# DLRM tower on one core: the first 32 samples prepared tile by tile with factors from TensorE, gathers and weight loads reordered

## What is computed

```python
def _cin_layer(X0, Xi, W, b):            # W: (128, 39 * Fi)
    Wr = W.reshape(H, F0_, Fi)
    return jnp.einsum('hjk,bjd,bkd->bhd', Wr, X0, Xi) + b[None, :, None]
Xi = X0 = e
for W, b in Ws:                          # three layers of 128 maps
    Xi = _cin_layer(X0, Xi, W, b)
    res.append(Xi.sum(axis=2))
z = jnp.concatenate(res, axis=1)         # (512, 384)
h = jnp.concatenate([z, dense_ctx], axis=1)
h = jnp.maximum(h @ W_top1 + b_top1, 0.0)   # 400 x 512
h = jnp.maximum(h @ W_top2 + b_top2, 0.0)   # 512 x 256
y = h @ W_top3                              # 256 x 1
```

## Time and profile before

| | |
|---|---|
| median of 3 runs | 688.73 us (688.02 to 689.34) |
| the profiled execution | 685.9 us, span 684.0 us, mean granted clock 0.99 |
| PE / PEld busy | 94% / 74% |
| DVE / ACT / POOL busy | 82% / 65% / 68% |
| HBM read | 8.86 MB |

### The profile page before, as it was taken

One profiled execution on the slowest core, in us unless ns is written; L12 is line 12 of the kernel. 1 busy time (PEld: TensorE's weight loads), 2 busy tenths in 40 slices (PEclk: granted clock), 3 DMA queues, 4 the chain that ended last, 5 costly groups with the idle time before them and its releaser, 6 DMA issues.

```text
span 684.0 us, 10984 instructions
## 1 busy us (share of the span) xinstructions
PE 641.0 (94%) x2920; PEld 507.6 (74%) x2920; DVE 558.1 (82%) x1560; ACT 441.3 (65%) x1434; POOL 464.6 (68%) x372
## 2 busy tenths in 40 slices
PE   0069999999999999999999999999999999999997
PEld 0037777777778877777788877877778887777877
DVE  4149999999994599999995589999997489999860
ACT  4026877777773477777684477778685377777751
POOL 6746888888874478787886368787886377444440
PEclk9999999999999999999999999999999999999988
DMA  6146424031312102213131200403040300300000
GB/s 217 41 128 242 149 67 122 11 109 24 97 36 80 52 3 56 79 35 99 27 107 27 95 13 18 115 19 115 18 117 16 102 17 14 117 2 5 1 1 1
DMA packets 39057, 44.35 MB, mean 65 GB/s; under 512 B 17427, under 2 KB 22253, under 8 KB 38867
## 3 DMA queue, kind: packets, MB, share of 16 engines
q1 hardware_dynamic: 33363, 42.34, 20.3%
q0 software_dynamic: 5632, 1.31, 2.1%
HBM read 8.86 MB, written 0.00 MB: 13 GB/s over the span
## 4 chain that ended last, share of the span: by engine, by line
PE 92%; DMA 2%; POOL 2%; SPq 1%; ACT 1%; issue 1%; DVE 1%; DVEq 0%
PE p_u L606 22%; PE p_u L608 21%; PE p_u L607 21%; PE p_tower L625 6%; PE p_x L583 6%; PE p_g L616 5%; PE p_x L580 2%; PE p_x L577 2%; PE p_x L578 2%; POOL emb L277 2%; PE p_tower L652 1%; DMA fac_b<-xx 1%; PE p_tower L638 1%; PE p_tower L637 1%; PE p_x L562 1%
## 5 line engine op out<-in xcount | busy, mean ns | idle before, releaser
L362 ACT ACTIVATE prod<-p_u,x0t 128x128 f32<-128x128 f32 x1024 | 289.3, 375 | 91.3 <-PE p_u L608 91.0
L496 DVE SCALAR_TENSOR_TENSOR parts<-p_u,x0t,parts 128x128 f32<-128x128 f32 x1024 | 283.0, 339 | 41.5 <-PE p_u L608 41.5
L606 PE MATMUL p_u<-w1h,x1h 128*128 128x512 f32 (+1 forms) x640 | 286.6, 448 | 2.3 <-DVE x1l L473 2.3
L608 PE MATMUL p_u<-w1h,x1l 128*128 128x512 f32 (+1 forms) x640 | 250.2, 391 | 0.0
L607 PE MATMUL p_u<-w1l,x1h 128*128 128x512 f32 (+1 forms) x640 | 249.9, 390 | 0.0
L277 POOL DMA_INDIRECT emb<-table_in,idx_all x176 | 204.5, 1162 | 51.4 <-issue 47.8
L296 POOL TENSOR_TENSOR parts<-parts,prod 128x512 f32<-128x512 f32 x128 | 176.3, 1378 | 57.8 <-ACT prod L362 44.2
L606 PEld LDWEIGHTS p_u<-w1h,x1h 128*128 128x128 f32 x640 | 121.0, 189 | 38.4 <-issue 9.7
L607 PEld LDWEIGHTS p_u<-w1l,x1h 128*128 128x128 f32 x640 | 121.6, 190 | 35.4 <-issue 10.1
L291 POOL TENSOR_TENSOR parts<-prod 128x512 f32<-128x512 f32 x64 | 83.6, 1306 | 86.8 <-ACT prod L362 86.1
L608 PEld LDWEIGHTS p_u<-w1h,x1l 128*128 128x128 f32 x640 | 120.6, 188 | 26.1
(11 more groups left out here) (56 smaller groups left out, 346.9 us busy)
## 6 DMA issues: line engine op xcount, KB each, us to landing
fac_b<-xx SPq DMA_DIRECT2D x96, 234.0 KB
fac_a<-xx SPq DMA_DIRECT2D x48, 78.0 KB
emb<-table_in,idx_all POOLq DMA_INDIRECT x176, 2.8
g_all<-w_in SPq DMA_DIRECT2D x3, 832.0 KB, 9.6
xx<-xx SPq DMA_DIRECT2D x32, 78.0 KB
fac_b<-xx SPq DMA_DIRECT2D x16, 156.0 KB
w<-w_in SPq DMA_DIRECT2D x1, 2496.0 KB, 10.2
bd<-x0t SPq DMA_DIRECT2D x128, 10.0 KB
```

The costliest lines, as they stand in the source:

```text
L362: last = nc.scalar.activation(dst[:, i * H:(i + 1) * H], u[:, i * H:(i + 1) * H], ACT.Copy, scale=x0t[:, par, t, j:j + 1])
L496: nc.vector.scalar_tensor_tensor(out=chain[i][:, p], in0=u[:, i * H:(i + 1) * H], scalar=x0t[:, par, t, j:j + 1], in1=add, op0=ALU.mult, o ...
L606: nc.tensor.matmul(u, xh, wh, start=True, stop=False)
L608: nc.tensor.matmul(u, xl, wh, start=False, stop=True).then_inc(u_full, 1)
```

## The change

Group 0 is prepared one tile at a time, and in another sample order (gather g holds samples 3g, 3g + 1, 3g + 2 of the group in its three parts, so that three gathers complete the first tile). TensorE moves the rows (`first_x0_rows`) and makes the factors by matmuls with selection matrices `rep`, `rep_a` (`first_factors`); DVE multiplies straight out of PSUM (`first_products`), and layer 0 runs on 128 columns in plain fp32 (`first_layer0`). Tile 0 is prepared ahead of the loop, tile t + 1 at fixed quads of tile t. The identity and the selection matrices are loaded from ACT's queue. W1 is asked for once the first three gathers have landed, in parts from its end, and the quads of a tile run through the fields from the end.

Group 1 is prepared at slots 30 to 39 of group 0, all in plain fp32. Group 2's gathers go into the loop: 6, 5, 3, 4 behind the four tiles of group 0, three behind each tile of group 1, then 3, 3, 3, 2. `bd` of group 0 is filled in two steps. The top network's weights are asked for after `spread(2)` and `place_bd(1)`. The context is loaded in group 0's sample order, and `y` is put back into order by three more copies.

The core of the diff:

```diff
+FIRST_PARTS = [range(0, 3), range(3, 6), range(6, 8), range(8, GATHERS)]
+F_X0, F_X0_OUT, F_PICK, F_PICK_OUT, F_XT_OUT, F_LAYER0, F_X1 = 0, 1, 3, 4, 5, 7, 7
+F_G = 8
+F_S_COLUMNS = 30
+F_S_PAIR = [30 + k for k in range(GROUPS)]
+F_S_ADD = [32 + k for k in range(GROUPS)]
+F_S_X1, F_S_X1L, F_S_Z1 = 38, 39, 31
+F_S_W0 = 16
+GATHER_ORDER = [(M, g) for M in range(2, MACROS * BLOCKS) for g in range(GATHERS)]
+GATHER_QUOTA = [6, 5, 3, 4] + [3] * 4 + [3, 3, 3, 2] * (MACROS * BLOCKS - 2)
-QUAD_J = [list(range(36, 39))] + [list(range(4 * q, 4 * q + 4)) for q in range(9)]
+QUAD_J = [list(range(36, 39))] + [list(range(4 * q, 4 * q + 4)) for q in reversed(range(9))]
...
             sp.dma_start(base[:], base_d).then_inc(idx_in, 16)
-            sp.dma_start(eye[:], eye_d).then_inc(eye_in, 16)
             sp.dma_start(fac_b[:].rearrange("p k c -> p (k c)")[:, 0:2 * GROUPS * H], w0_d).then_inc(w0_in, 16)
+            sp.wait_ge(first_in[0], 16 * len(FIRST_PARTS[0]))
             step = F * H // W1_PARTS
             for i in range(W1_PARTS):
+                c = slice((W1_PARTS - 1 - i) * step, (W1_PARTS - i) * step)
+                sp.dma_start(w1_raw[:, c], w1_d[:, c]).then_inc(w1_in[i], 16)
-            spread(0, 0, first=True)
+            sp.wait_ge(bd_cleared, 1)
+            sp.wait_ge(f_xt_made, 2)
+            place_first_bd(0, f_bd_in)
             spread(1, 1)
+            sp.wait_ge(f_xt_made, TILES)
+            place_first_bd(2, bd_in[0])
             over_blocks(body)
...
             pool.wait_ge(idx_made, 1)
-            for M in (0, 1):
-                for g in range(GATHERS):
-                    gather(M, g)
-            for g in range(8):
-                gather(2, g)
+            for t in range(TILES):
+                for g in FIRST_PARTS[t]:
+                    gather(0, g, first_in[t])
+            for g in range(GATHERS):
+                gather(1, g, gathered[1])
...
+            def first_x0_rows(t):
+                for i in range(t + 1):
+                    pe.wait_ge(first_in[i], 16 * len(FIRST_PARTS[i]))
+                need(pe, f_x1f_made, t)
+                o = p_x1[0:F, t * 128:(t + 1) * 128].rearrange("p (s d) -> p s d", d=D)
+                for c in range(STACK):
+                    last = nc.tensor.matmul(o[:, s0:TILE_B:STACK, :], eye[0:(c + 1) * F, c * F:(c + 1) * F],
+                                            emb[0:(c + 1) * F, 0, g0 * D:g1 * D].rearrange("p (g d) -> p g d", d=D),
+                                            start=True, stop=True)
+            def first_factors(t):
+                x0 = first_x0[:, t * 128:(t + 1) * 128]
+                pe.wait_ge(f_x0_made, t + 1)
+                need(pe, f_z_made, 2 * t)
+                nc.tensor.matmul(p_x1[0:ROWS, t * 128:(t + 1) * 128], rep_a[:], x0,
+                                 start=True, stop=True).then_inc(f_a_full, 1)
+                for k in range(GROUPS):
+                    last = nc.tensor.matmul(o, rep[:, k:k + ROWS], x0, start=True, stop=True)
+                    if k in (3, GROUPS - 1):
+                        last.then_inc(f_b_full, 1)
+                pe.wait_ge(f_a_made, t + 1)
+                nc.tensor.transpose(p_x1[:, t * 128:t * 128 + F], x0, eye[0:F, 0:F]).then_inc(f_xt_full, 1)
+            def first_layer0(t):
+                pe.wait_ge(f_xt_made, t + 1)
+                for k in range(GROUPS):
+                    if k in (0, 4):
+                        pe.wait_ge(f_z_made, 2 * t + (2 if k else 1))
+                    rows = GROUP_ROWS[k]
+                    last = nc.tensor.matmul(p_x1[:, t * 128:(t + 1) * 128], w0[0:rows, k * H:(k + 1) * H],
+                                            first_z0[0:rows, k, :], start=(k == 0), stop=(k == GROUPS - 1))
+                last.then_inc(f_l0_full, 1)
...
+            def first_products(t):
+                dve.wait_ge(f_a_made, t + 1)
+                need(dve, f_l0_full, t)
+                for bank, ks in ((p_g, range(0, 4)), (p_tower, range(4, GROUPS))):
+                    dve.wait_ge(f_b_full, 2 * t + (2 if ks[0] else 1))
+                    nc.vector.tensor_tensor(out=first_z0[:, ks[0]:ks[0] + n, :],
+                                            in0=bank[0:ROWS, 0:n * 128].rearrange("p (k c) -> p k c", c=128),
+                                            in1=fac_a[:, 0:1, c].to_broadcast([ROWS, n, 128]),
+                                            op=ALU.mult).then_inc(f_z_made, 1)
...
+            first_columns(0)
+            first_factor(0)
+            first_x0t(0)
+            w1_high(0)
+            w1_high(1)
+            first_x1(0)
+            w1_high(2)
...
+            first_products(0)
+            w1_low(0)
+            first_x1l(0)
+            w1_low(1)
+            w1_low(2)
...
+            first_x0_rows(0)
+            pe.wait_ge(rep_a_made, STACK)
+            first_factors(0)
+            pe.wait_ge(w0_summed, 1)
+            first_layer0(0)
             over_blocks(body)
```

317 lines of the change are left out of this document (215 added, 102 removed).

## The result

The changed kernel takes 683.94 us in the median of 9 runs (680.01 to 687.67), the kernel before 688.73 on the same chip (9 runs, 687.58 to 689.34). The ratio is 0.9935, 95% interval 0.991 to 0.9961: faster by 4.8 us, where 11.7 were forecast. The runs of after spread over 7.7 us, those of before over 1.8. The profiled execution of after is the slowest of the nine, so it shows the losses at their largest. The ratios in this document leave out the few executions that took over 1.5% longer than the fastest of the same kernel; the medians are of all.

A forecast was written before the change was run, and what follows sets the result against it. TensorE bounds the steady groups, so only the 49 us head could be won. Group 1 at 72.5 instead of 84.73 gains 12.2: 685.9 - 12.2 + 0.5 = 674.2 profiled, 677.0 as median, range 671.5 to 684.5.

The forecast's parts named there:

- What bounds the kernel: Whole kernel: TensorE has no gap from 84.73 us on, groups take 35.35; only the 49 us head can be won.
- rival (b): Group 0: TensorE bounds it, small matmuls cost up to 0.41 us, group 1 starts at 75 to 80.5, 680 to 685; chance 0.17.
- The prediction's own signs of being wrong: First quad after 25 us, tiles 1 and 2 over 14, clock of 20 to 70 below 0.9, or later groups over 35.4.
- Start of the quads: Head: W1's transfer and rounding set quad 0 at about 18.9 us instead of 49.06, bounds 18 and 21.
- The price of the small matmuls: Group 0: 0.22 us each, plus 0.8 us per tile for possible mode changes, 4.7 us per tile taken.
- 1.5 for a start at half clock: Tile 0 of group 0: 1.5 us added for a cold start, from 3 us at clock 0.50; tile 0 13.1.
- rival (e): Group 0: clock stays low; over 14.2 us lost makes the kernel slower, 694.5 us with 20 us of work at half clock; chance 0.06.
- Tile 3: Last tile of group 0: 13.8 us with seven unsplit fp32 groups of 0.86, plus about 1 us at the end.
- The feed of group 2: Group 2's eleventh gather starts at 58.9, first product at 75.0; TensorE stands unless group 1 starts at 72.2 or later.
- rival (a): The forecast itself: group 1 starts at 70 to 75 us, PE stands 1 to 3 in quad 6, 674.5 to 680; chance 0.50.
- The weights of the top network: Asked for at 83 us behind group 2's transfers, over at 93.4, at a group 3 gather's issue; 0.5 us put for it.
- Rival (d): Top network's weights delay group 3's last gather by 4.4 us, a stall of 3.4, 679.9 us; chance 0.10.

The follow-up runs named there:

- the probe: Kernel before, with sixteen more 128-column matmuls per tile, of 39 rows in groups 9 and 10, of 117 in 13 and 14; a tile grew by 3.9 and 3.5 us.
- fillers: Filling matmuls on zeros added to the changed kernel ahead of tile 0 (682.8 us) or of every tile of group 0 (682.04 us); also combined with other versions.
- the kernel strewn in group 0 alone: Changed kernel with group 0's gathers spread between GpSimd's sums, 16 ahead of the loop; 676.36 us, on another chip 676.13.
- the unchanged kernel: The changed kernel as it is, run again on the second chip where the kernel before takes 684 us: 674.24 us, ratio 0.9854.
- kernels with strewn gathers: Changed kernel with gathers spread between GpSimd's sums: in group 0 alone, 0.9893; throughout, with filling matmuls ahead of tile 0, 1.0136.
- the selection in one pass: Changed kernel with the selection matmuls in fp32r, one pass instead of two, rounding the rows of the first 32 samples; 680.75 us, ratio 0.9904.

## Why the prediction was right and wrong

**What bounds the kernel: right.** The head was what there was to win, group 1 stayed at 35.3 us, and all that stands behind group 0 took 600.5 us against 601.2.

**The median: inside the stated bounds by luck.** 683.94 is 6.9 us over the forecast 677.0, and the gain is 4.8 of 11.7. It lies where rival (b) put it, but (b)'s price wasn't there; what filled the gap is below. The prediction's own signs of being wrong came: in the first profile tile 1 exceeds 14 us, and the clock of 20 to 70 is 0.86.

**Start of the quads: 20.84, forecast 18.9, bounds 18 to 21.** W1 was taken for the bound, and it wasn't: ScalarE is through with the second third at 18.48 and then waits 0.5 us for TensorE. TensorE's own steps were the bound, "9.1 to about 16.5" in the prediction and 9.85 to 18.95 here. The chain of waits shows them in the profile of the second 684 chip, where every update is on record (quad 0 at 20.3):

```profile
6.61 2.84 DMA emb<-table_in,idx_all
...
11.65 1.71 PE p_g L725 x8
...
15.04 3.34 PE p_x L737 x14
...
19.54 0.79 PE p_x L711 x6
20.32 0.62 PE p_u L797
```

The third gather lands 2.84 us after its start (3.05 in after), not 2.33. The small matmuls run at half clock, 0.43 us each, those of layer 0 0.48; the 0.22 of the prediction is their price at full clock. And the rows of tile 1 (0.79) stand ahead of quad 0, which the sum leaves out. The selection matrices, put at nothing "under gathers 1 to 3", did no harm: they landed at 9.20 in after, ahead of the third gather (9.72), and `rep_a` was ready at 9.71 and used at 11.16.

**The price of the small matmuls: right, at either end of the clock.** The chain of after, tile 0's selection at full clock and tile 1's at half (eight pieces are four matmuls, six are three):

```profile
25.44 0.93 PE p_g L725 x8
26.36 0.66 PE p_tower L725 x6
...
44.55 1.71 PE p_g L725 x8
46.26 1.28 PE p_tower L725 x6
```

0.22 to 0.23 us each, and 0.43 at half. Rival (b)'s 0.41 for alternating shapes isn't there at full clock. A tile at full clock has 11.4 to 11.5 us of work, forecast 11.6. The rule of the Trainium skill that a change of tiling mode drains the engine ("TensorEngine Tiling (Array Packing)", Key Properties) left nothing that shows beside 0.22 here: in the probe a matmul of 39 rows cost 0.02 us more than one of 117, and no run tells whether the mode changed at all.

**Tile 0, the step that failed: "1.5 for a start at half clock".** The row of 3 us at 0.50 was taken for the length of every such start. By the distance of the starts, the quads ran at half clock for 3 to 4 us in five of the eleven profiles without fillers (the first among them), for 9 in one and for 12 in five. Where it was 3 us and no update was late, tile 0 took 13.0 and 12.8 us, the forecast 13.1 (the kernel strewn in group 0 alone). Where it was 12, in the unchanged kernel without late updates, it took 17.4, so the short term cost 4.3 us. What makes it last the one or the other wasn't found. In the long ones tile 1's selection matmuls of 39 rows (24.1 to 27.9 in this profile) lie inside the slow stretch, and in the probe the clock fell beside such matmuls; that the two belong together isn't shown. With fillers it took 11.4 in two profiles of five, with no half clock in it, which shows the clock as the cause; the other three have a low clock or late updates in tile 0 again, and 13.0 to 17.5 us.

**What no term had: late updates.** On the chip of the result, and on the three others where the kernel before takes 688, each of ten profiles with group 0 in its new form had updates late while group 0's quads ran, the latest by 2.5 to 7.1 us. In the first profile that was 5.3 us of standing in tile 0, and then half clock over most of tile 1: 17.1 against 11.6. That is the step the prediction doesn't have: its group 0 goes without a wait between TensorE and the engines that read its results, but for 1 us at the end. The end is rival (e)'s, given 0.06, a group 1 that starts later than before, but not by (e)'s clock alone. (e) wanted 14.2 us lost to the clock. The clock was at half for 17.0 us (39.1 to 52.7 and 73.2 to 76.6), which loses about 8.5 (an estimate, half of 17.0); TensorE stood for 5.3 us in tile 0 and 2.9 in tile 3. In the median run all this took only a part of the gain. (e)'s chance was weighed by the shape of the matmuls; in this profile the long fall follows directly on TensorE standing for 5.3 us.

**Tile 3: 18.4, forecast 14.8; 15.7 without late updates.** VectorE, not in the sum, was behind at the first product of group 1; this is TensorE's wait in after:

```profile
72.37 1.23 PE L772 MATMUL p_x<-z,w 117*128 117x512 f32 x2 [2.12 <-DVE z L589]
```

The same wait is 1.05 us in the undisturbed kernel. In after, the clock fell for 3.4 us behind it (73.2 to 76.6). The prices of the fp32 groups were right: 13.83 us of PE work, forecast 13.8.

**The feed of group 2: the mechanism right, and hidden where TensorE was late.** SP's queue in after:

```profile
69.34 2.48 SPq L251 DMA_DIRECT2D xx<-emb  x3
...
79.07 5.60 SPq L268 DMA_DIRECT2D fac_b<-xx  x7
```

Here the last round is issued at 79.07, its first part has landed at 82.27, and with group 1 at 87.2 nobody waits for it. The spread began 8 us later than forecast, 5.6 of them because the eleventh gather starts at 64.54 instead of 58.9, the rest because `place_first_bd(2)`, which stands ahead of it on SP, waited for tile 3's `x0t` until 64.08. In the unchanged kernel without late updates the eleventh gather starts at 57.90 and the first `fac_b` has landed at 75.72, forecast 75.0; group 1 starts at 77.5 and doesn't wait. And where group 1 started at 72.87 and 71.84, in two kernels with strewn gathers, TensorE stood in quad 6 for 1.6 and 2.0 us and tile 4 took 12.4 and 12.5 us instead of 8.5, which is rival (a)'s picture. So both bounds were real, 2 us apart as forecast; TensorE's moved from 70.5 to 77.5 and 87.2.

**The weights of the top network: 0.5 forecast, nothing seen.** They were asked for at 90.39. Group 3's first `fac_b` transfer was issued at 119.36, 5 us before its product was wanted (2.3 after 122.48). Rival (d) didn't occur. The Trainium skill's rule on the order of completion ("DMA: Bandwidth & Descriptors", Queues, rings and completion order) is neither borne out nor spoken against by this. Group 3's last gather was issued at 107.31, 15 us after the last big transfer of weights, and its spread began 2.3 us later.

**The sum.** Terms over the forecast for the first profile: 1.9 (quad 0), 6.0 (tile 0), 5.5 (tile 1), -0.3 (tile 2), 3.6 (tile 3), 16.7 in all, which is 87.2 - 70.5. For the kernel on the second 684 chip: 1.4, 4.3, 0.4, 0 and 0.9, 7.0 in all. The slowest of the runs was profiled in both; by the medians and the same 600.5 us group 1 starts at 83.4 and 73.7 (an estimate). On the second kind of chip the change gives 9.7 us, near the forecast 11.7; on the first kind 4.8 and 7.1.

**What stays open.** What sets the two kinds of chip apart; the kernel before differs by 4 us between them, and no profile of it was taken on the faster kind. The late update in the probe's head moved the first quad by 2.5 us, so it may be a part of these 4, and of the 2.8 us by which the median of before lies above its profile; that is argued from one profile, not shown. That a run of eleven gathers makes updates late is shown on one chip; plain transfers in their place took the late updates out of tile 0 in one profile. Whether strewing alone does it on such a chip wasn't seen, nor whether eleven in a row in every group would do harm on a 684 chip. By which way the gathers hold the updates back isn't visible in a trace. Whether it is the gathers' being indirect, GpSimd's being busy or the traffic was separated by no run. How the gain on a 688 chip divides between late updates and half clock in the median execution isn't known, as none near the median was profiled in the comparison. No version beats the changed kernel: the lowest ratio of all is its own 0.9854, and none that ran beside it has an interval wholly below its interval.

## What to carry to other kernels

Don't take one short row for the length of a start at half clock: here it lasted 3 to 4 us in some executions of the same work and 12 in others. Give it a range, and read the distance of equal matmuls' starts. A wait inside dense work can cost twice, once as itself and once as the half clock behind it; so a head that is filled with many dependent small steps gains less than its gap.

Long runs of indirect gathers beside a busy TensorE are a risk of their own. Three in a row cost no time here, but strewing more of them between GpSimd's sums delayed the gathers of the group after next, and TensorE then waited for that group. Two bounds that lie 2 us apart have both to be kept: a cure for one brings out the other. And take the comparison on more than one chip before a gain of 1% is told as a number.

## What the runs showed of the hardware

- TensorE's semaphore updates came up to 7.1 us after the last matmul they stand for, several at once, some 50 ns apart, in all 11 profiles with long runs of gathers beside quads on chips where the kernel before takes 688 us, and in none of 7 profiles on chips where it takes 684. The waiting engine's row says "remote". With eleven gathers in a row, the held updates begin to come 1.5 to 1.9 us after the last of them has ended, 13 times of 13.
- Runs of three gathers on such chips showed updates up to 1.4 us late beside the top network's matmuls (377.9 to 379.3 in the profile of the selection in one pass), with no time lost on TensorE.
- A start from idle ran at half clock for 3 to 4 us of quads in five profiles, 9 in one and 12 in five; the column of the granted clock says 1.00 over it.
- Small matmuls of 39 rows let the clock fall (0.83 over 31 us) with PE busy without a gap; those of 117 rows didn't (1.00 over 30 us).
- A matmul of 39 rows and 128 columns in plain fp32 takes 0.22 to 0.24 us at full and 0.43 at half clock; one of 117 rows takes 0.22 at full clock.
- Three transfers of the context with samples three apart took 5.86 us together to issue on SP's queue, against 0.4 to 0.9 for each of the others of the top network.
